# Four attention layers on one core: GpSimd issues part of the moves into the stacked queries and keys

## The reference

```python
attn = jnp.einsum('bqd,bkd->bqk', q * scale, k)
rel_h = jnp.einsum('bhwc,hkc->bhwk', qr, Rh)
rel_w = jnp.einsum('bhwc,wkc->bhwk', qr, Rw)
bias = rel_h[..., :, None] + rel_w[..., None, :]
attn = jax.nn.softmax(attn + bias.reshape(B * nh, N, N), axis=-1)
```

## Time and profile before

| what | value |
|---|---|
| median of 3 runs | 178.74 us (178.67 to 179.8) |
| the profiled execution | 178.91 us |
| its span in the profile | 177.1 us |
| TensorE (PE) busy | 162.6 us, 92% of the span, 1020 matmuls |
| VectorE / ScalarE / GpSimd busy | 87.2 / 69.6 / 35.1 us |
| granted clock of TensorE | 0.998 of full speed |
| GpSimd's DMA queue (software) | 2.05 MB, 3248 packets |
| SP's DMA queue (hardware) | 12.08 MB, 9952 packets |

### The profile page before, as it was taken

One profiled execution on the slowest core, in us unless ns is written; L12 is line 12 of the kernel. 1 busy time (PEld: TensorE's weight loads), 2 busy tenths in 40 slices (PEclk: granted clock), 3 DMA queues, 4 the chain that ended last, 5 costly groups with the idle time before them and its releaser, 6 DMA issues.

```text
span 177.1 us, 2779 instructions
## 1 busy us (share of the span) xinstructions
PE 162.6 (92%) x1020; PEld 104.3 (59%) x1020; DVE 87.2 (49%) x223; ACT 69.6 (39%) x157; POOL 35.1 (20%) x61
## 2 busy tenths in 40 slices
PE   7899969999979998999989998999999899699992
PEld 2488627655434766655438755666665588276550
DVE  2444438846335687745370024384344444088462
ACT  4243303772214125772145523346632053127820
POOL 7851048410892053005000000000000000000000
PEclk9999999999999999999999999999999999999999
DMA  4999972998139053000000000620000016330001
GB/s 115 264 259 202 188 175 77 271 306 214 7 16 178 6 153 111 0 0 4 0 0 0 0 0 4 187 79 2 4 0 0 0 64 179 103 103 4 0 2 44
DMA packets 13662, 14.71 MB, mean 83 GB/s; under 512 B 3760, under 2 KB 11952, under 8 KB 13632
## 3 DMA queue, kind: packets, MB, share of 16 engines
q1 hardware_dynamic: 9952, 12.08, 27.3%
q0 software_dynamic: 3248, 2.05, 7.7%
q10 hardware_dynamic: 448, 0.39, 0.8%
HBM read 7.96 MB, written 0.20 MB: 46 GB/s over the span
## 4 chain that ended last, share of the span: by engine, by line
PE 59%; SPq 13%; DVE 11%; ACT 6%; DMA 4%; issue 4%; POOL 1%; DVEq 0%; ACTq 0%; POOLq 0%
SPq L302 13%; PE PC L945 12%; PE RING L810 7%; PE RING L919 7%; PE PB L956 6%; PE RING L878 4%; DMA QS<-RL 3%; PE RING L1117 3%; PE PA L1123 3%; PE PA L1015 2%; PE PA L894 2%; PE PC L942 2%; PE PB L878 2%; DVE QHL L711 1%; PE PB L984 1%
## 5 line engine op out<-in xcount | busy, mean ns | idle before, releaser
L810 PE MATMUL RING<-WARM 128*128 128x512 bf16 x139 | 36.8, 397 | 1.3 <-POOL WARM L356 1.3
L548 ACT ACTIVATE PR<-RING 128x512 f32<-128x512 f32 (+1 forms) x48 | 25.3, 555 | 11.2 <-PE RING L919 10.9
L945 PE MATMUL PC<-PR,VX 128*32 128x256 f32 (+1 forms) x192 | 23.3, 367 | 0.0
L733 DVE TENSOR_REDUCE NM<-RING 128x2 fp32r<-128x512 f32 (+1 forms) x32 | 20.1, 653 | 5.7 <-PE RING L878 5.5
L810 PEld LDWEIGHTS RING<-WARM 128*128 128x128 bf16 x139 | 12.9, 102 | 14.4 <-issue 2.2
L919 PE MATMUL RING<-QS,KS 128*128 128x256 f32 (+1 forms) x96 | 18.5, 297 | 0.9 <-ACT QS L540 0.5
L919 PEld LDWEIGHTS RING<-QS,KS 128*128 128x128 f32 x96 | 13.6, 189 | 7.3 <-issue 4.9
L733 DVE TENSOR_REDUCE NM<-PB 128x2 fp32r<-128x512 f32 (+1 forms) x16 | 10.5, 654 | 10.1 <-PE PB L878 10.0
L945 PEld LDWEIGHTS PC<-PR,VX 128*32 128x32 f32 x192 | 9.6, 109 | 8.1 <-ACT PR L548 1.3
L740 DVE STREAM_TRANSPOSE TURNED_U<-PC 128x256 f32<-128x256 f32 x12 | 5.4, 450 | 15.9 <-PE PC L945 15.9
L878 PE MATMUL RING<-KS,QS 128*128 128x256 f32 (+1 forms) x64 | 12.2, 290 | 0.3 <-DMA QS<-RL 0.3
(11 more groups left out here) (161 smaller groups left out, 248.8 us busy)
## 6 DMA issues: line engine op xcount, KB each, us to landing
WQKV<-in_w SPq DMA_DIRECT2D x2, 576.0 KB, 7.9
WO<-in_wo SPq DMA_DIRECT2D x4, 288.0 KB, 9.5
QS<-QHL SPq DMA_DIRECT2D x18, 64.0 KB, 4.7
W<-in_ff SPq DMA_DIRECT2D x2, 576.0 KB, 7.8
WQKV<-in_w SPq DMA_DIRECT2D x2, 432.0 KB, 6.3
KS<-in_hot POOLq DMA_DIRECT2D x4, 192.0 KB, 9.4
KS<-KH SPq DMA_DIRECT2D x4, 192.0 KB, 5.8
QS<-RH SPq DMA_DIRECT2D x12, 64.0 KB, 2.0
```

The costliest lines, as they stand in the source:

```text
L548: A(PR[:, h % NPR, 0:n], exponents(l, h)[:, 0:n], ACT.Exp).then_inc(sem("probs"), 1)
L733: V.tensor_reduce(NM[1 if h < EARLY else g % 2][:, :, h % GH], MAXIMA[h % 3][:, 0:2 * n_keys].rearrange("p (q k) -> p q k", q=2), AX.X, AL ...
L810: M(bank, WARM[:, 0:P], WARM[:, :], start=True, stop=True)
L945: ins = M(columns(h)[:, reach(l, k)], VX[:, k, h, :], half(PR[:, h % NPR, :], l, k), start=(k == 0 and l != 2), stop=(k == 1), skip_group_ ...
```

## The change

SP no longer issues the query moves of heads 4 to 11 in layers 0 and 3, nor the high keys of the second half in layers 1 and 2. GpSimd issues them: in layer 0 after it has scaled the keys' part of the weights of layer 2, in layer 3 after it has cleared the top rows of the stack, in layer 1 after its low part of the queries, in layer 2 as soon as the keys are there. The sets of bytes moved and their sources and destinations stay the same. TensorE waits for them by semaphores of their own.

```diff
@@ sync
                     for i in range(NC):
                         heads = slice(i * HPC, (i + 1) * HPC)
                         for block in (Q_HIGH, Q_AGAIN):
                             move("qh", rows_of(queries, block)[:, heads], QH[:, i, :], "later heads" if i else "q stack", i + 1)
-                        if i:
-                            for block in (Q_HIGH, Q_LOW):
-                                move("kh", rows_of(KS, block, KEY0, REG1)[:, heads], KH[:, i, :], "later heads", i + 1)
                         move("ql", rows_of(queries, Q_LOW)[:, heads], QL[:, i, :], "later heads" if i else "q stack", i + 1)
...
                 high_queries(0)
                 low_queries(0)
-                high_queries(1)
                 for block in (Q_HIGH, Q_LOW):
                     move("kh", rows_of(KS, block, KEY0, REG1), KH[:, :, :], "k stack")
                 move("kl", rows_of(KS, Q_AGAIN, KEY0, REG1), KL[:, :, :], "k stack")
-                high_queries(2)
-                low_queries(1)
-                low_queries(2)
                 for g in range(NG):
                     for w in range(2):
                         for name, block, src in (("rel h", ROW_HIGH, RH), ("rel l", ROW_LOW, RL)):
...
-                    sync.wait_ge(*upto("third heads", 0, 7 * 16))
+                    sync.wait_ge(*upto("third heads", 0, 4 * 16))
                     load(later_loads)
@@ gpsimd
             scale_keys("w2", WQKV[2])
 
+            def move_later_keys(l):
+
+                pool.wait_ge(*upto("kh", l, NC))
+                for block in (Q_HIGH, Q_LOW):
+                    pool.dma_start(rows_of(KS, block, KEY0, REG1)[:, HPC:NH].bitcast(F32), KH[:, 1, :].bitcast(F32))\
+                        .then_inc(sem("later keys"), 16)
+
             for l in range(LAYERS):
                 if l >= 2:
 
                     pool.wait_ge(*upto("scores", l - 2, NH))
                     g.memset(QS[l % 2][0:GH, :, :].bitcast(F32), 0.0).then_inc(sem("rows clear"), 1)
+                if l in REL_LAYERS:
+
+                    for group, done in ((1, "second queries"), (2, "third queries")):
+                        heads = slice(group * GH, (group + 1) * GH)
+                        pool.wait_ge(*upto("qh", l, group + 1))
+                        for block in (Q_AGAIN, Q_HIGH):
+                            pool.dma_start(rows_of(QS[l % 2], block)[:, heads].bitcast(F32), QHL[0:64, group, :].bitcast(F32))\
+                                .then_inc(sem(done), 16)
+                        pool.wait_ge(*upto("ql", l, group + 1))
+                        pool.dma_start(rows_of(QS[l % 2], Q_LOW)[:, heads].bitcast(F32), QHL[64:128, group, :].bitcast(F32))\
+                            .then_inc(sem(done), 16)
+                if l == 2:
+                    move_later_keys(2)
                 if l == 0:
...
                     pool.wait_ge(*upto("qh", 1, 2))
                     g.tensor_tensor(QL[:, 1, :], QF[:, 1, :], QH[:, 1, :].bitcast(F32), ALU.subtract).then_inc(sem("ql"), 1)
+                    move_later_keys(1)
@@ tensor, for_maxima
                 if h == HPC and l not in REL_LAYERS:
-                    pe.wait_ge(*upto("later heads", l, 6 * 16))
+                    pe.wait_ge(*upto("later heads", l, 4 * 16))
+                    pe.wait_ge(*upto("later keys", l, 2 * 16))
                 if h in (GH, 2 * GH) and l in REL_LAYERS:
-                    pe.wait_ge(*upto("second heads" if h == GH else "third heads", l, 7 * 16))
+                    which = "second" if h == GH else "third"
+                    pe.wait_ge(*upto(f"{which} heads", l, 4 * 16))
+                    pe.wait_ge(*upto(f"{which} queries", l, 3 * 16))
```

More of the change, by code:

```diff
@@ L262, in build @@
                     "qh": {0: NG, 1: NC, 2: NC, 3: NG}, "ql": {0: NG, 1: NC, 2: NC, 3: NG},
-                    "q stack": {l: (7 if l in REL_LAYERS else 3) * 16 for l in range(LAYERS)}, "later heads": {l: 6 * 16 for l in (1, 2)}}
+                    "q stack": {l: (7 if l in REL_LAYERS else 3) * 16 for l in range(LAYERS)}, "later heads": {l: 4 * 16 for l in (1, 2)}, "later keys": {l: 2 * 16 for l in (1, 2)}}
         signals |= {"x": {l: 3 * NC if l == 1 else NC for l in range(LAYERS)}, "sums": {0: 1}}
         signals |= {name: {l: count for l in REL_LAYERS} for name, count in {
-            "rel psum": 4, "rel h": 4, "rel l": 4, "second heads": 7 * 16, "third heads": 7 * 16}.items()}
+            "rel psum": 4, "rel h": 4, "rel l": 4, "second heads": 4 * 16, "third heads": 4 * 16,
+            "second queries": 3 * 16, "third queries": 3 * 16}.items()}
         signals |= {name: {t: count for t in (1, 3)} for name, count in {
```

## The result

| | before | changed |
|---|---|---|
| median | 178.7 us (4 runs, 177.96 to 179.8) | 176.6 us (4 runs, 176.25 to 179.12) |
| profiled execution | 178.91 us | 176.29 us |
| its span | 177.1 us | 174.5 us |

The ratio is 0.986, 95% interval 0.981 to 0.991: faster, by 1.4% instead of the 2.1% forecast. Medians here are over all runs, and every ratio leaves out those in the chip's occasional slower state. 176.6 us lies inside the range and 1.7 us above the number. It is close to the number of the first rival, 176.4.

A forecast was written before the change was run, and what follows sets the result against it. TensorE was taken to stand 4.05 us waiting for moves, chiefly because SP issued them late. Gains of 1.5 + 0.55 + 0 + 1.75 = 3.8 us gave 175.1 profiled, 174.9 for the runs; range 174.1 to 176.8.

The forecast's parts named there:

- the first rival: Layer 0: the DMA backlog decides, relative rows again land at 26.5, layer 0 gives 0; 176.4 us, chance 0.1.
- the first two rivals: Layer 0 held by DMA backlog (176.4 us, chance 0.1); GpSimd's keys late in layer 1 (176.0 us, chance 0.1).
- Layer 3, 1.75 us: Layer 3, heads 0 and 4: SP issues relative rows late; without its query moves 1.75 us are gained.
- TensorE starts at 153.21: Layer 3, head 0: starts when the kept-warm block of matmuls ends, so the whole 1.57 us wait goes, not more.
- issued at 153.6, lands at 155.6: Layer 3, head 4: the second group's last relative row begins at about 153.6 and lands 2.0 us later.
- Layer 1, 0.55 us: Layer 1, head 6: low key lands earlier and GpSimd's high keys arrive just in time; gain 0.55 us.
- The rivals about GpSimd's queue: GpSimd's keys land late in layer 1: needing 4.5 us (176.0 us, chance 0.1) or 9.4 us (180.9 us, chance 0.04).
- the third rival: Layer 1: GpSimd's queue is slow, moves take 9.4 us, possibly held by DVE's two-port modes; 180.9 us, chance 0.04.
- Layer 2, nothing: Layer 2, head 6: the low key comes 1.27 us earlier but nothing waited for it; gain 0.
- Layer 0, 1.5 us: Layer 0, head 0: starts at 25.05 instead of 26.56 once SP issues the relative rows earlier; gain 1.5 us.
- the end of the backlog, behind which the relative rows can land at once: Layer 0: start's loads and moves are worked off at about 25.0; relative rows land then if issued by 20 or so.
- RL landed 3.6 us after a late issue while the share fell to 0.58, so there was room at the end: Layer 0: argument that DMA engines had room for earlier relative rows, against the backlog deciding (176.4 us, chance 0.1).

The follow-up runs named there:

- the two others above: Changed kernel with layer 0's six queries back on SP, 176.43 us; and with only layer 3's queries moved to GpSimd, 178.12 us.
- the experiments: Changed kernel with layer 0's queries back on SP (ratio 0.983 to before), against only layer 3's queries moved to GpSimd (0.994).
- relative rows held: Changed kernel, but in layer 0 SP waits before the second group's relative rows until the first group has landed; 177.38 us (1 run).
- lean start: Changed kernel, with wo0 and HOT (416 KB) loaded later and layer 0's third-group queries (192 KB) issued after the first group landed; 174.5 us.
- 288 KB earlier: Changed kernel, with layer 1's output weights (288 KB) loaded at the end of the start instead of later; 178.33 us.
- lean order on SP alone: Changed kernel, SP issuing all layer 0 moves, later groups' queries behind earlier groups' relative rows, wo0 and HOT loaded later; 178.08 us.

## Why the prediction was right and where it failed

The number fell into the range, but not by the reckoning: of the 3.8 us summed, 2.6 came, and the range held them because it had been stretched to the first two rivals. The forecast's own bounds ended at 176.2.

- **Layer 3, 1.75 us: right, with 1.9 in this trace and 1.5 in the two others above.** The cause was SP's list, as read: with six moves gone, the last relative row is issued right behind DVE's. SP and DVE of the changed kernel:

```profile
149.54 0.55 SPq L303 DMA_DIRECT2D QS<-RH  x1
150.13 0.59 SPq L303 DMA_DIRECT2D QS<-RL  x1
```

```profile
149.54 0.55 DVE L736 TENSOR_TENSOR RL<-RING,RH 64x384 fp32r<-64x384 f32 x1 [0.38 <-ACT RH L536]
```

  What was off is "TensorE starts at 153.21". Head 0 did not wait for the whole modelled length of the kept-warm block: it began 1.63 us after its start, not 1.90. So 1.84 us went by there, above the bound of 1.57. (SP came to the first relative row sooner than the 147.88 of the forecast, since two of the six moves stood ahead of the keys; nothing hung on that row.) Head 4 has not quite lost its wait. Its last row was issued at 152.68 and lands 2.0 later, 154.7, where the head starts (154.78): the estimate "issued at 153.6, lands at 155.6" was right to 0.2 us after the shift by layer 1.
- **Layer 1, 0.55 us: right, and 0.2 too small.** KL was issued at 66.49 (66.46 forecast). GpSimd's keys landed 2.4 us after their issue, less than the 3.3 taken, so there was room:

```profile
KS<-KH POOLq DMA_DIRECT2D x2, 96.0 KB, 2.4
```

  The wait itself was all that the 0.55 counted; the layer gave 0.75 in the profile and 0.6 to 0.79 between the experiments, and where the rest comes from wasn't followed up. The rivals about GpSimd's queue have fallen: its moves landed after 2.4 us on quiet queues, against 2.0 to 2.5 for SP's, and its issues took 0.51 to 0.57 each. The hold by DVE that the third rival named did not show in layer 1: the two issues took 1.08 us from 65.43, beside a TENSOR_TENSOR of DVE until 65.66 and its reductions from 65.81.
- **Layer 2, nothing: right.** From layer 1's output projection to its own it takes 50.70 us instead of 50.71.
- **Layer 0, 1.5 us: wrong, it gave 0.** The failed step is "the end of the backlog, behind which the relative rows can land at once". It took the end of the backlog (25.05) from the trace of before, where SP was late and its later relative rows followed from 23.5 on (22.89 and a step of 0.64; now from 19.85), and held it fixed, "whoever issued them". It isn't fixed. In the changed kernel the share was 1.08 from 24 to 25 and 0.76 from 25 to 26, the key landed at 25.67 and the row, issued at 19.22, at 26.5. With 192 KB of GpSimd's 384 KB taken away it landed at 25.5, and with 608 KB less in all head 0 had no wait. So what shares the engines with the first group counts. How much of it is due to SP's later relative rows, which come sooner too (64 KB each 0.64 us), stays open: holding them back moved head 0 by 0.4 in one profile, less than the scatter. Second, even a backlog that ends at 25.0 does not release TensorE at 25.0 but, in the run with the relative rows held, at 26.12.
- **The argument against the rival was misread.** "RL landed 3.6 us after a late issue while the share fell to 0.58, so there was room at the end" is true of a late issue only. The room was there because the issue was late. The key's 10.1 us were the better row: a move issued at 15 was still on its way at 25, and took 10.8 in the changed kernel, where more was issued behind it.
- The rule quoted from the Trainium skill ("DMA: Bandwidth & Descriptors", section "Issuing engines are not separate DMA queues") was borne out: a second issuer saved the time of issuing, 2.6 us where the queues were quiet, and nothing at a share of 1.09. It had earned more than a chance of 0.1.

Not tried: a shorter kept-warm block in layer 0 on top of the lean start, and a different order of the second group's rows in layer 3, where head 4 is still met by its move.

## What to carry to other kernels

Ahead of a wait for a DMA, read two numbers: when it was issued against when its data were ready, and how long it took to land against the same move on quiet queues (2.0 us here). Where only the first is late, another issuer brought it all (layers 1 and 3); where the share was at 1, issuing sooner traded one wait for the other, and what helped was to take out bytes that stood ahead (608 KB for 1.9 us of head 0 here). Never keep the end of a backlog fixed when the change is what fills the queues.

## What the hardware showed that was not expected

The same program had head 0 of layer 0 at 26.52, 27.15 and 27.49. In all three the last relative row of the first group was issued at about 19 (19.22, 18.81 and 19.13), but it took 7.3, 8.3 and 8.3 us to land: 26.5, 27.1 and 27.4. The DMA engines had moved less in the slower two: 177 and 169 GB/s from 16 to 24, against 200, at a share of 1.19 to 1.24 in all three. Why the same list moves its bytes at different rates, these runs do not show.

The clock of TensorE is a second thing to see there. In the second run TensorE stood 0.77 us before the kept-warm block, and then the granted clock was 0.51, the 1.2 GHz level, from 22 to 24, and 18 matmuls took 5.73 us instead of 4.05:

```profile
21.59 5.73 PE L825 MATMUL PB<-WARM 128*128 128x512 bf16 x18 [0.77 <-issue]
```

```profile
22.00:24.00 2.00, 2.00 (x6) 0.71 (x5) 1.70 (x9) 0.00 (x0) 0.00 (x0) 0.51 1.08 250
```

It cost next to nothing: head 0 began at 27.15, right behind the row's landing at 27.1. The run with 288 KB earlier shows the same (0.72 us idle, then 0.50 and 5.73 us). In the lean order on SP alone it did cost: around the wait at head 8 TensorE was busy 0.58 us of two, and the clock fell behind it.

```profile
30.00:32.00 2.00, 0.58 (x4) 0.41 (x5) 0.70 (x2) 0.78 (x2) 0.00 (x0) 1.00 0.20 66
32.00:34.00 2.00, 2.00 (x12) 1.58 (x13) 1.39 (x2) 1.16 (x3) 0.21 (x1) 0.52 0.58 134
34.00:36.00 2.00, 2.00 (x11) 1.00 (x8) 0.15 (x1) 0.50 (x2) 1.70 (x4) 0.63 1.03 299
```

But such a gap does not always cost the clock. The third time of the changed kernel stood 1.17 us there, and its clock stayed at 1.00. With the relative rows held, TensorE was even less busy at head 4, 0.44 us of the two from 28 to 30, and the clock was 1.00 in the next two as well.

```profile
22.31 4.04 PE L825 MATMUL PB<-WARM 128*128 128x512 bf16 x18 [1.17 <-issue]
```

What tells these cases apart, the runs do not show. For the reader it means that a DMA that comes late at a matmul can cost more than its wait.
